# Sorted tiles made of two independent half tiles of 128 rows, and a lead of four token groups instead of five, in a two-layer graph network with a mixture of experts

## Reference, cut to what matters

```python
x = x + gnn(layernorm(x), edges, edge_type, ...)        # two relational layers, x is 10000 x 512
t = layernorm(x)
hs = gelu(einsum('td,nfd->ntf', t, sw1) + sb1)          # 2 shared experts, F = 64
shared = einsum('ntf,ndf->td', hs, sw2) + sb2.sum(0)
probs = softmax(t @ gate_w.T + gate_b)                  # 8 routed experts
top_v, top_i = top_k(probs, 2)
cw = zeros_like(probs).at[arange(T)[:, None], top_i].add(top_v)
hr = gelu(einsum('td,efd->etf', t, rw1) + rb1)
routed = einsum('etd,te->td', einsum('etf,efd->etd', hr, rw2) + rb2, cw)
return x + shared + routed
```

## Time and profile before

| | us |
|---|---|
| median of 3 runs (lowest, highest) | 1600.99 (1600.15, 1612.06) |
| the profiled execution's own time | 1598.47 |
| its span, first to last instruction | 1596.7 |
| TensorE busy | 1491.6 (93%) |
| VectorE busy | 927.9 (58%) |
| ScalarE busy | 705.7 (44%) |
| GpSimd busy | 662.6 (41%) |

### The profile page before, as it was taken

One profiled execution on the slowest core, in us unless ns is written; L12 is line 12 of the kernel. 1 busy time (PEld: TensorE's weight loads), 2 busy tenths in 40 slices (PEclk: granted clock), 3 DMA queues, 4 the chain that ended last, 5 costly groups with the idle time before them and its releaser, 6 DMA issues. The chain is left out here.

```text
span 1596.7 us, 27768 instructions
## 1 busy us (share of the span) xinstructions
PE 1491.6 (93%) x8680; PEld 1200.0 (75%) x8680; DVE 927.9 (58%) x2667; ACT 705.7 (44%) x1231; POOL 662.6 (41%) x989
## 2 busy tenths in 40 slices
PE   6999998989898999999999986599999999999997
PEld 4777666777786677777888864478888888888986
DVE  5555686867752333334766556566666767665453
ACT  3334334556652212122666535446565656453322
POOL 3762232457753000000467634546546464543222
PEclk9999999999999999999999998699999999999999
DMA  9999999597757999999667688879776776534220
GB/s 243 277 279 286 298 294 304 190 289 131 128 91 170 295 290 279 278 292 272 157 126 133 106 214 175 236 204 249 224 233 191 221 213 200 167 129 131 93 75 3
DMA packets 130212, 325.95 MB, mean 204 GB/s; under 512 B 17115, under 2 KB 17641, under 8 KB 129698
## 3 DMA queue, kind: packets, MB, share of 16 engines
q1 hardware_dynamic: 84626, 211.19, 44.8%
q0 software_dynamic: 45456, 113.12, 31.1%
HBM read 205.62 MB, written 121.74 MB: 205 GB/s over the span
## 5 line engine op out<-in xcount | busy, mean ns | idle before, releaser
L1207 ACT ACTIVATE th<-bank 128x512 fp32r<-128x512 f32 x158 | 94.2, 597 | 291.7 <-PE bank L1487 291.6
L1005 POOL DMA_INDIRECT gx<-y,dst_slot x42 | 46.2, 1101 | 266.1 <-ACT xn_e L1227 243.0
L1842 DVE SCALAR_TENSOR_TENSOR tl<-bank,th 128x512 fp32r<-128x512 f32 x79 | 54.4, 689 | 162.3 <-ACT th L1207 162.0
L1139 POOL DMA_INDIRECT out<-xt,out_row x90 | 93.2, 1035 | 128.4 <-DVE xt L2198 92.3
L1467 PE MATMUL bank<-root2h,th 128*128 128x512 f32 x316 | 133.1, 421 | 12.6 <-DVE tl L1842 7.8
L1467 PE MATMUL bank<-root1h,th 128*128 128x512 f32 x316 | 131.6, 416 | 7.9 <-DVE yout L1869 4.8
L1869 DVE TENSOR_TENSOR yout<-bank,bias_b 128x512 f32<-128x512 f32 x150 | 102.3, 682 | 45.4 <-DMA y<-yout 18.7
L1467 PE MATMUL bank<-root2l,th 128*128 128x512 f32 x316 | 126.0, 399 | 0.0
L1467 PE MATMUL bank<-root2h,tl 128*128 128x512 f32 x316 | 125.2, 396 | 0.0
L1467 PE MATMUL bank<-root1l,th 128*128 128x512 f32 x316 | 125.0, 396 | 0.0
L1467 PE MATMUL bank<-root1h,tl 128*128 128x512 f32 x316 | 124.1, 393 | 0.0
(11 more groups left out here) (355 smaller groups left out, 4378.8 us busy)
## 6 DMA issues: line engine op xcount, KB each, us to landing
basis_t<-in_gnn_basis SPq DMA_DIRECT2D x64, 896.0 KB
xt<-sorted_rows SPq DMA_DIRECT2D x45, 560.0 KB, 3.9
xin<-in_x SPq DMA_DIRECT2D x39, 512.0 KB, 8.8
xin<-y SPq DMA_DIRECT2D x39, 512.0 KB, 8.5
y<-yout SPq DMA_DIRECT2D x37, 512.0 KB, 9.2
z<-yout SPq DMA_DIRECT2D x34, 512.0 KB, 8.4
stage1q<-in_x SPq DMA_DIRECT2D x5, 1024.0 KB, 7.5
stage2q<-in_x SPq DMA_DIRECT2D x5, 1024.0 KB, 8.7
```

The costliest lines, as they stand in the source:

```text
L1005: pool.indirect_dma_start(out=gx[:, e % 6, :], out_offset=None, in_=x if pr.phase == SB else y1, in_offset=bass.IndirectOffsetOnAxis(ap=ds ...
L1139: pool.indirect_dma_start(out=out, in_=xt[i % 4][:, j, 0:H], in_offset=None, out_offset=bass.IndirectOffsetOnAxis(ap=out_row[:, i % 4, j:j ...
L1207: act.activation(th_a[:, s, :], tpb[s][:], f).then_inc(s_hi, 1)
L1842: ins = dve.scalar_tensor_tensor(out=tl_a[:, s, :], in0=tpb[s][:], scalar=0.0, in1=th_a[:, s, :].bitcast(F32), op0=ALU.max, op1=ALU.subtract)
```

## The change

The tile keeps 256 rows but is made of two halves of 128 rows, each with a kind, a start row and weights of its own. Kinds are filled up to multiples of 128 rows, which makes `NF` = ((10000 + 6 x 127) // 128 + 1) // 2 = 42. `pick_tile` chooses twice, the loading engines read two sets of numbers, each tile comes in by two DMAs of 128 rows, and `weigh` works on one half at a time. The lead has four groups, tile 0 is picked behind group 1, `stage4q` and the wait for it are gone, and all offsets of the main loop are smaller by two slots. Groups now ride in slots 0 to 31; slots 32 to 41 carry tiles alone.

```diff
-    KIND = FW + N
+    KIND = P + N
-    NF = (N + NKIND * (FW - 1)) // FW
+    NF = ((N + NKIND * (P - 1)) // P + 1) // 2
-    LEAD_GROUPS = 5
+    LEAD_GROUPS = 4
-            return min(NQ - 1, (i + 5) // 2)
+            return min(NQ - 1, (i + 3) // 2)
...
-                r = sp.value_load(pick_int[0:1, i, 0:1], min_val=0, max_val=XROWS - FW)
-                sp.dma_start(xt[i % 4][:], sorted_rows[bass.ds(r, FW), :].rearrange("(p j) w -> p j w", j=2))\
-                    .then_inc(s_xt[i % 4], 16)
+                for j in range(2):
+                    r = sp.value_load(pick_int[0:1, 2 * i + j, 0:1], min_val=0, max_val=XROWS - P)
+                    sp.dma_start(xt[i % 4][:, j, :], sorted_rows[bass.ds(r, P), :]).then_inc(s_xt[i % 4], 16)
...
             load_group(4)
+            sp.wait_ge(s_pads, 16 * NKIND)
+            load_tile(0)
             load_group(5)
-            sp.wait_ge(s_pads, 16 * 2 * NKIND)
-            load_tile(0)
+            load_tile(1)
             load_group(6)
-            load_tile(1)
-            load_group(7)
-            sp.wait_ge(s_sorted[0], 16 * QT * 2)
             load_tile(2)
...
-                return [pe.value_load(pick_int[0:1, i, c:c + 1], min_val=int(c > 1), max_val=tops[c - 1]) for c in (1, 2, 3)]
+                return [[pe.value_load(pick_int[0:1, 2 * i + j, c:c + 1], min_val=int(c > 1), max_val=tops[c - 1])
+                         for c in (1, 2, 3)] for j in range(2)]
...
-                slot, chunks = chosen[0], chosen[1:]
+                chunks = [row[1:] for row in chosen]
                 for j in range(2):
-                    ins = up_routed(i, j, slot)
+                    ins = up_routed(i, j, chosen[j][0])
...
-                down_routed(i, 0, chunks)
+                down_routed(i, 0, chunks[0])
                 if exists(i + 1):
                     turn_tile(i + 1, "x")
                     chosen = picked(i + 1)
-                down_routed(i, 1, chunks)
+                down_routed(i, 1, chunks[1])
...
-                link(dve.tensor_reduce(pick[:, i, :], pick_all[:], AX_X, ALU.add))
-                dve.tensor_copy(pick_int[0:1, i, :], pick[0:1, i, 0:4])
+                dve.tensor_reduce(pick[:, n, :], pick_all[:], AX_X, ALU.add)
                 link(dve.tensor_tensor(last, last, pick_all[:, 5, :], ALU.add))
+
+            def pick_tile(i):
+
+                q = group_of_pick(i)
+                dve.wait_ge(s_qpos, q + 1)
+                for j in range(2):
+                    pick_half(2 * i + j, q)
+                link(dve.tensor_copy(pick_int[0:1, 2 * i:2 * i + 2, :], pick[0:1, 2 * i:2 * i + 2, 0:4]))
                 dve.sem_inc(s_pick, 1)
...
-                dve.tensor_tensor(part, part, share.to_broadcast([P, 2, 2, P // 2]), ALU.mult).then_inc(s_gs, 1)
+                dve.tensor_tensor(part, part, share.to_broadcast([P, 2, P // 2]), ALU.mult).then_inc(s_gs, 1)
...
-                chunks = [dve.value_load(pick_int[0:1, i, c:c + 1], min_val=1, max_val=FC - 1) for c in (2, 3)]
-                for c in range(2):
-                    weigh(i, c, chunks[c])
+                chunks = [[dve.value_load(pick_int[0:1, 2 * i + j, c:c + 1], min_val=1, max_val=FC - 1) for c in (2, 3)]
+                          for j in range(2)]
+                for c, j in itertools.product(range(2), range(2)):
+                    weigh(i, c, j, chunks[j][c])
```

More of the change, by code:

```diff
@@ L286, in gnn_moe_kernel @@
         xt3, x5 = place("xt3", [P, 2, XW], at=x4)
-        stage4q, x6 = place("stage4q", [P, QT, XW], at=x3)
-        assert x6 == x5
-        stage = (stage1q, stage2q, stage0q, stage3q, stage4q)
+        stage = (stage1q, stage2q, stage0q, stage3q)
         xt = (xt0, xt1, xt2, xt3)
@@ L562, in stage_of @@
         def stage_of(q):
-            return stage[q if q < LEAD_GROUPS else (q - 1) % 4]
+            return stage[q % 4]
         def stage_free(eng, q):
[L568 to L573, removed]
+            wait(eng, s_sorted[q % 4], 16 * QT * (q // 4))
         def tiles_of(q):
@@ L610, in picked_in_slot @@
                 return [t for t in (i + 3, i + 4) if t < NF]
-            return [i + 4] if i > 2 * NQ - 10 and i + 4 < NF else []
+            return [i + 4] if i > 2 * NQ - 8 and i + 4 < NF else []
         def logit_bank(q):
-            return bank[1] if q in (1, 3) else bank[7]
+            return bank[1] if q in (0, 2) else bank[7]
         def rank_bank(q):
@@ L824, in _ @@
             for k in range(NKIND):
-                for j in range(2):
-                    first = HEAD + k * KIND + j * P
-                    sp.dma_start(sorted_rows[first:first + P, :], zeros[:]).then_inc(s_pads, 16)
+                first = HEAD + k * KIND
+                sp.dma_start(sorted_rows[first:first + P, :], zeros[:]).then_inc(s_pads, 16)
             walk(sp, SC, step)
@@ L870, in _ @@
                     load_tile(i + 3)
-                if group_at(i, 15) is not None and group_at(i, 15) > 7:
-                    load_group(group_at(i, 15))
+                if group_at(i, 13) is not None and group_at(i, 13) > 6:
+                    load_group(group_at(i, 13))
             for i in range(4):
@@ L1151, in _ @@
                 add_z(q)
-            for q in range(4):
-                if q == 3:
-                    add_z(4)
+            for q in range(3):
                 group_rstd(q)
@@ L1178, in _ @@
                     rows_of_tile(i + 1)
-                if group_at(i, 11) is not None and group_at(i, 11) > 5:
-                    group_rstd(group_at(i, 11))
+                if group_at(i, 9) is not None and group_at(i, 9) > 4:
+                    group_rstd(group_at(i, 9))
                 if 0 < i <= len(LATE2_PAIRS) + 1:
@@ L1452, in _ @@
                     q_exp(q_route)
-                q = group_at(i, 11)
-                if q is not None and q > 5:
+                q = group_at(i, 9)
+                if q is not None and q > 4:
                     q_norm(q)
@@ L1710, in _ @@
             logits(0)
[L1711 to L1719, removed]
+            q_transpose(1, 0)
+            q_transpose(1, 1)
+            logits_by_token(0)
+            q_transpose(1, 2)
+            q_transpose(1, 3)
+            logits(1)
+            logits_by_token(1)
+            count_ranks(0)
+            q_transpose(2, 0)
+            q_transpose(2, 1)
+            count_ranks(1)
+            q_transpose(2, 2)
+            q_transpose(2, 3)
+            logits(2)
             logits_by_token(2)
-            count_ranks(1)
             count_ranks(2)
+            for part in ("a", "b", "x"):
+                turn_tile(0, part)
             turn_group(3)
@@ L2231, in _ @@
             sort_kinds(1)
+            positions(1)
+            pick_tile(0)
+            q_stats(3, range(QT))
             route_a(2)
-            positions(1)
+            for n in range(FC + E_SPLITS, SPLITS):
+                expert_lo(n)
             route_b(2)
@@ L2264, in _ @@
                 routed_lo(i)
-                if q_more is not None and q_more > 5:
+                if q_more is not None and q_more > 4:
                     q_stats(q_more, range(2, QT))
@@ L2273, in _ @@
                     pick_tile(t)
-                if q_first is not None and q_first > 5:
+                if q_first is not None and q_first > 4:
                     q_stats(q_first, range(2))
```

114 lines of the change are left out of this document (45 added, 69 removed).

## The result

| | us |
|---|---|
| before, median of 4 runs (lowest, highest) | 1602.89 (1600.15, 1612.06) |
| after, median of 4 runs (lowest, highest) | 1656.22 (1646.30, 1660.03) |
| ratio of the two, 95% interval | 1.031 (1.025 to 1.038) |
| forecast (range) | 1650 (1622 to 1685) |
| the profiled execution of after, time and span | 1654.12, 1652.4 |

The account below looks back on a forecast made before the run. TensorE was taken to set the pace. From 1598.5 us: -28.7 tiles, -5 and -4 lead and slot 1, +83.9 loads, +2 VectorE, +5 clock gives 1651.7, taken as 1650; range 1622 to 1685.

Parts of the forecast that it names:

- The three added loads: TensorE's register loads at line 1737: three fit beside issued matmuls, three more cost 1.85 to 2.35 us a slot, 83.9 us.
- The clock: TensorE's granted clock falls to 0.50 behind some of the longest holes only: three falls at 1.6 us, 5 us.
- The two windows: TensorE's clock fell to 0.50 after 1.31 of 3.30 us busy, stayed at 1.00 after 1.44 of 3.40.
- most holes: Rival: TensorE's clock falls behind most holes in the loop, 40 to 66 us in place of 5, about 1700; 10%.
- the bound that I gave for being wrong: Sign against the forecast: TensorE's granted clock in the loop below 0.95.
- Fewer tiles: Expert loop: 15 group pairs and 15 slots alone become 16 pairs and 10 alone, -28.7 us.
- The lead: Before slot 0: two scattered groups for tile 0 instead of three, -5 us; slot 1's wait for its tile gone, -4.
- Four pieces less bring tile 0 forward by 5.1 us: Lead: tile 0's load waits for four fewer scatter pieces of 1.3 us each; -5 us taken, bounds 0 and -10.
- VectorE: One more choice per tile and two more register loads, mostly beside TensorE's matmuls: 2 us charged.
- my rival: VectorE's four loads of 0.9 us end behind the gelu in slots with two picks: +16 us, 1666; 10%.
- Hidden: Rival: TensorE's issuer runs ahead far enough for six loads, which stay hidden: 1563 us; 5%.
- half price: Rival: TensorE's added loads overlap and cost 0.3 us each, 37 us: 1600 us, no change; 5%.

Follow-up runs that it names:

- the row loads: Kernel after, with one register load into four registers for each half's four numbers, on TensorE and VectorE: 1552.8 us, 0.9702 of the kernel before.
- the two runs: One register load per half on TensorE and VectorE in the kernel after: 0.9702; 45 undivided 256-row tiles, four-group lead, one such load a slot on each: 0.9929.
- the moved loads: Kernel after with one TensorE load per half's numbers; VectorE's four single loads for the next tile moved ahead of f_lo in the slot before: 1604.3 us, 1.0036.

## Why the prediction was right, term by term

**The three added loads: price and place were right.** Forecast 83.9 us, 1.85 to 2.35 a slot. The idle time booked to "issue" behind the start of slot 0 is 79.4 - 3.6 = 75.8 us against 3.3 - 1.6 = 1.7 before, so 74 us more; measured slot by slot from the end of the x transposes to the start of the next matmul it is 82.5 against 3.6, 79 us more. A slot alone is 1.98 us longer. The reading that three loads use up the reserve and three more come on top was tested both ways, by three added to the old kernel and three taken from the new one, and by the row loads, with which the holes are gone.

**The clock: the term that was mis-sized most.** Forecast three falls, 5 us; there were twelve, 20 us. The two windows were there to read, a hole of 2.35 us in 16 slots was forecast too, and I still took "some of the longest holes only, three". It was not the case of "most holes" (41 falls) either: behind the single slots' 1.7 us the clock stayed at 1.00, but for the last. Pairs came to 30.8 us on average instead of 30 for this reason. In the loop the clock was 0.96, above the bound that I gave for being wrong. Loads and clock together: forecast 88.9, read 94 to 99, and by the ratios 1.0345 - 0.9702 = 6.4%, some 103 us, where VectorE is in time.

**Fewer tiles.** -28.7, in line with the two runs: 36 us for the half tiles, less the 4 us (25.8 - 2 x 10.9) by which the lead lengthens the loop, are 32.

**The lead: -5 and -4.** Slot 0 began 8.7 us earlier, 3.7 more than taken, though still inside the bounds. The step that failed is "Four pieces less bring tile 0 forward by 5.1 us", taken for the whole gain: the load of tile 0 was issued at 1000.99, not 1015.84. Of these 14.9 us the four pieces are 5.4 (from 1002.54 to 1007.98 in the trace of before). The other 9.2 lie ahead of the first scatter, for which GpSimd waits until VectorE has written group 0's positions. Its timeline there, before and after:

```profile
992.35 0.23 POOL L1115 TENSOR_SCALAR stage1q<-token_base 128x4 f32<-128x4 f32 x1 [3.67 <-DVE pos L2156]
983.11 0.23 POOL L1108 TENSOR_SCALAR stage1q<-token_base 128x4 f32<-128x4 f32 x1 [3.94 <-DVE pos L2140]
```

The prediction named this path (group 3's statistics "no longer stand ahead of group 0's routing on VectorE") and gave it no price. The statistics are some 2.4 us of it (the step that they interrupt, from 983.00 to 985.94 before, goes from 977.95 to 978.50); another 4.7 are there already when VectorE does its last addition for the layers before (972.97, not 977.66), and why, like the rest, is left open. At TensorE less arrives: it waited 10.09 us for tile 0, ahead of group 3, began it 10.2 us earlier than before, and went on to the logits of group 3 before slot 0. The wait in slot 1 went, as forecast.

**VectorE: 2 us charged, 2.0 us read** (its gelr late in three slots). The amount was right. Of the two covers that I named, the longer slots hold, by TensorE's holes; the 58% of busy time does not. With the holes gone VectorE costs 1.6%, 26 us, more than the 16 us of my rival: I had priced its loads at 0.9 us as the dearest, and they took up to 1.7.

**Sum.** Slot 0 starts 8.7 us earlier. For the loop, the terms of tiles and slot 1 as forecast and those of holes and clock as read give -28.7 - 4 + 74 to 79 + 20 = 61 to 66, against 63.8 measured from the first slot's start to the last one's; the rest is +0.6. That is 55.7 us more span. The path was the forecast one, but that the sum came within 6 us of the median is in part luck: the clock term, 15 too small, and the lead and load terms, 4 and 5 to 10 too dear, partly cancelled.

**The rivals.** "Hidden" fell with the 42 holes, and "half price" with the first row of line 1720, 0.64 us from load to load. The rule of the Trainium skill that other instructions can be read and queued while a control instruction executes (Advanced Engine Details and Errata, Sequencer Loop) did not help TensorE here beyond what had been issued ahead of the loads: 42 holes. A figure that I should have weighed is that of DMA: Bandwidth & Descriptors (Latency and other measured facts), which puts the floor of a `tensor_load` at about 600 ns; the trace agrees, with 0.64 us from one to the next, where the load itself lasts 0.30. By the page 41 x 1.8 = 74 us, an estimate.

## What to carry to other kernels

Price a register load by its spacing (0.64 to 0.8 us here, with its two register operations), per engine, and ask at each place how much issued work covers it: up to that cover loads are free, beyond it each costs its full spacing, plus the clock behind long holes. Load neighbouring numbers with one instruction (two row loads a slot turned a loss of 3% into a gain of 3%). When one limit is removed, look at once for the next that it hid, and if loads must move, move them off the chain that the slot waits on.

## What the runs showed of the hardware

- **One load, four registers: 0.34 us, against 0.30 for one.** Eight numbers took 0.59 us at least. The Trainium skill (Runtime: NRT & Kernel Launch, Instruction fetch mechanics) gives about 200 ns for each register, in bulk too, for the loads that the runtime adds, from HBM; by it four would take 0.8 us, an estimate. The loads of these runs come from on-chip memory, and the trace has less than half of that.
- **The same load takes 0.30 us or up to 1.7.** In the kernel with three loads on TensorE, the 60 of VectorE's 168 loads that start 0.5 to 9 us behind the issue of `add_z` (a DMA that accumulates 1 MB of z into the group's buffer on the chip) last 0.99 us on average, the other 108 last 0.31. The split was drawn after the fact, and it is not the whole rule: the four loads of slot 0, 4.4 to 6.3 us behind such an issue, took 0.31, and in the kernel before 28 loads on the near side took 0.47 against 0.34. The issue ahead of the slow loads shown above, in the timeline:

```profile
1220.80 1.36 POOL L1098 DMA_DIRECT2D stage2q<-z  x1
```

  And in the view of DMAs, with KB and us to landing:

```profile
stage2q<-z POOLq DMA_DIRECT2D x1, 1024.0 KB, 8.5
```

  The expectation for the moved loads had it that busy DMA engines are the cause. That is not enough: in the same trace (columns as in the windows above):

```profile
1210.30:1212.50 2.20, 2.02 (x24) 1.88 (x23) 1.48 (x3) 2.18 (x3) 0.00 (x0) 1.00 0.96 351
1222.40:1227.30 4.90, 4.89 (x39) 3.71 (x38) 2.47 (x4) 1.29 (x2) 3.65 (x7) 1.00 0.97 160
```

  The first window has the short loads, the second the slow ones, both at a DMA share of 0.96 or more. What differs is what is moved. Moving the loads away from that DMA shortened them; whether it is the accumulation that delays them was not tried and stays open.
